# Stacking the split projections by 32 KB transfers within SBUF instead of through a DRAM scratch

## The reference, cut to what matters

```python
x = x + 0.5 * moe(layernorm(x))            # 8 experts, top 2, capacity 193
x = x + attention(layernorm(x))            # 16 heads of 8, causal, ALiBi, biases
x = x + 0.5 * moe(layernorm(x))

# attention, per sequence (S = 512, H = 16, HD = 8)
q, k, v = x @ Wq + bq, x @ Wk + bk, x @ Wv + bv
scores = einsum('bthd,bshd->bhts', q, k) / sqrt(HD) + alibi     # -inf above the diagonal
out = einsum('bhts,bshd->bthd', softmax(scores), v) @ Wo + bo
```

## Time and profile before

| | |
|---|---|
| median of 3 runs (lowest, highest) | 1023.84 us (1015.57, 1025.05) |
| the profiled execution: its time, its span | 1020.61 us, 1018.9 us |
| mean granted TensorE clock, of full speed | 0.893 |
| busy: TensorE, VectorE, ScalarE, GpSimd | 869.3, 756.3, 634.8, 537.1 us |
| all DMA | 92532 packets, 75.15 MB |
| scratch stores | x192, 128.0 KB, median 2.4 us from issue to landing |
| stack transfers | x64 each to `q_st`, `k_max`, `k_exp`, 192.0 KB, medians 3.8, 5.0 and 6.1 us |
| shift transfers | x64, 4.0 KB, median 4.0 us |

### The profile page before, as it was taken

How to read it: one execution, slowest core, us unless ns; L and a number is a source line. 1 busy time by engine, 2 the same in 40 slices (tenths; PEclk the granted TensorE clock), 3 DMA queues, 4 the chain that set the end, 5 groups by cost and what they waited for, 6 DMA issues and landing times. The chain is left out here.

```text
span 1018.9 us, 24637 instructions
## 1 busy us (share of the span) xinstructions
PE 869.3 (85%) x6498; PEld 396.8 (39%) x6498; DVE 756.3 (74%) x2534; ACT 634.8 (62%) x1538; POOL 537.1 (53%) x838
## 2 busy tenths in 40 slices
PE   4989995389798897898998988989989995998997
PEld 3444442143243343433433433433433433544443
DVE  5999984477776777778777777778777813799996
ACT  4676764007665575676676666666766783676765
POOL 3777775234453553544544544535535231677777
PEclk9999997557897898989988988988988997899999
DMA  6600000653644725535526436346247000011001
GB/s 170 95 0 0 0 0 1 155 120 77 116 98 70 147 61 96 132 66 112 121 67 122 105 68 137 89 81 140 76 80 155 2 2 22 11 31 31 27 25 42
DMA packets 92532, 75.15 MB, mean 74 GB/s; under 512 B 11540, under 2 KB 92308, under 8 KB 92308
## 3 DMA queue, kind: packets, MB, share of 16 engines
q1 hardware_dynamic: 92488, 74.63, 34.8%
HBM read 44.97 MB, written 29.36 MB: 73 GB/s over the span
## 5 line engine op out<-in xcount | busy, mean ns | idle before, releaser
L1099 DVE TENSOR_REDUCE att_neg_max<-att_max 128x1 bf16<-128x512 f32 (+3 forms) x704 | 416.3, 637 | 149.3 <-PE att_max L893 147.3
L992 ACT ACTIVATE att_probs<-att_exp 128x512 f32<-128x512 f32 x640 | 352.5, 600 | 201.2 <-PE att_exp L912 196.8
L1064 POOL TENSOR_SCALAR_AFFINE_SELECT att_probs<-att_probs 128x512 f32<-128x512 f32 x256 | 157.7, 638 | 272.1 <-ACT att_probs L992 272.1
L890 PE MATMUL att_max<-att_k_max,att_q_st 51*128 51x384 bf16 (+2 forms) x768 | 198.9, 304 | 56.4 <-DMA att_k_exp<-qk_parts 48.2
L912 PE MATMUL att_exp<-att_q_st,att_k_exp 64*128 64x512 bf16 (+3 forms) x1024 | 230.2, 326 | 4.8 <-DMA att_q_st<-att_shift 3.3
L928 PE MATMUL att_pv<-att_probs,att_v 128*32 128x512 f32 (+3 forms) x2048 | 216.2, 498 | 1.5 <-POOL att_probs L1064 1.5
L358 ACT ACTIVATE moe_scaled<-moe_hi,moe_gates 128x128 f32<-128x128 f32 x512 | 146.1, 372 | 60.6 <-PE moe_hi L304 60.3
L893 PE MATMUL att_max<-att_k_max,att_q_st 62*128 62x128 bf16 x1024 | 182.1, 233 | 0.0
L518 DVE SCALAR_TENSOR_TENSOR x<-moe_lo,moe_gates,x 128x128 f32 (+1 forms) x512 | 160.5, 338 | 19.5 <-PE moe_lo L298 18.4
L890 PEld LDWEIGHTS att_max<-att_k_max,att_q_st 51*128 51x128 bf16 x768 | 74.1, 99 | 253.8 <-DVE att_neg_max L1099 164.4
L298 PE MATMUL moe_lo<-moe_we,moe_hT 128*128 128x512 f32 x256 | 136.0, 614 | 0.0
(11 more groups left out here) (81 smaller groups left out, 892.2 us busy)
## 6 DMA issues: line engine op xcount, KB each, us to landing
qk_parts<-att_parts SPq DMA_DIRECT2D x192, 128.0 KB, 2.4
att_q_st<-qk_parts SPq DMA_DIRECT2D x64, 192.0 KB, 3.8
att_k_max<-qk_parts SPq DMA_DIRECT2D x64, 192.0 KB, 5.0
att_k_exp<-qk_parts SPq DMA_DIRECT2D x64, 192.0 KB, 6.1
x<-in_L_attn_x SPq DMA_DIRECT2D x16, 256.0 KB, 3.1
out<-x SPq DMA_DIRECT2D x16, 256.0 KB, 2.3
moe_we<-in_L_ffn_We SPq DMA_DIRECT2D x2, 512.0 KB, 4.6
att_q_st<-att_shift SPq DMA_DIRECT2D x64, 4.0 KB, 4.0
```

Of the source, the lines that this page charges most:

```text
L890: nc.tensor.matmul(max_ps[m % RING][:, at:at + width - P], q_st[par][low:low + FINE_ROW, r, i * P:(i + 1) * P], k_max[par][low:low + FINE_ ...
L992: nc.scalar.activation(probs[g % 2][:, n, :], exp_ps[m % RING][:], ACT.Exp).then_inc(exp_done, 1)
L1064: nc.gpsimd.affine_select(out=view, in_=view, compare_op=ALU.is_ge, fill=0.0, base=0, pattern=[[0, 4], [1, P]], channel_multiplier=-1).the ...
L1099: nc.vector.tensor_reduce(neg_max[par][:, g // 2, 1 - g % 2, heads[0]:heads[0] + len(heads), i], max_ps[m % RING][:, 0:len(heads) * width] ...
```

## The change

The DRAM tensor and `store_parts` go away. `stack` copies straight from `parts` to the stacks: for each half, each of the six terms, each stack and each of the two heads of a pair one transfer of 8 destination rows by 4 pairs by 512, read from 32 source rows, 36 per half and 72 per sequence. To make the 32 source rows of one half and one head of the pairs adjacent, the columns of Wq and Wk and their biases are handed over in another order. A first half waits for the split parts term by term; the first split of a sequence waits for the whole second half of the sequence before. The tables of slots are new: statistics and normalise of a sequence stand in group 3 of the step before, `turn_h`, projections and splits come earlier, `shift_hi` and `turn_o1` later. An extra step at -3 starts the first sequence.

```diff
--- before.py
+++ after.py
@@ -562,15 +562,17 @@
 
 
 SIDE_WORK = [
-    {2: "shift_hi"},
-    {1: "turn_h", 3: "turn_o1", 5: "project_q", 8: "project_k"},
-    {0: "turn_o", 3: "shift_lo", 6: "project_v"},
-    {1: "output", 3: "turn_o0"},
+    {3: "turn_h", 7: "project_q"},
+    {0: "project_k", 5: "shift_hi", 9: "turn_o1"},
+    {3: "turn_o", 7: "shift_lo"},
+    {0: "project_v", 4: "output", 9: "turn_o0"},
 ]
 
-PREPARE = {(0, 1): "statistics", (0, 2): "aggregate", (0, 3): "add_eps", (0, 4): "take_root", (0, 6): "shift_mean",
-           (0, 7): "normalise0", (0, 8): "normalise1", (0, 9): "normalise2", (0, 10): "normalise3", (1, 6): "split_q0", (1, 7): "split_q1", (1, 8): "split_q2", (1, 9): "split_q3",
-           (1, 10): "split_k0", (2, 0): "split_k1", (2, 1): "split_k2", (2, 2): "split_k3", (3, 4): "add_bias"}
+
+PREPARE = {(0, 10): "split_q0", (1, 0): "split_q1", (1, 1): "split_q2", (1, 2): "split_q3",
+           (1, 3): "split_k0", (1, 4): "split_k1", (1, 5): "split_k2", (1, 6): "split_k3", (2, 4): "add_bias",
+           (3, 0): "statistics", (3, 1): "aggregate", (3, 2): "add_eps", (3, 3): "take_root", (3, 6): "shift_mean",
+           (3, 7): "normalise0", (3, 8): "normalise1", (3, 9): "normalise2", (3, 10): "normalise3"}
 PV_AFTER = {3: 0, 5: 1, 7: 2, 9: 3}
 MAX_UNITS = 11
 EXP_UNITS = 10
@@ -657,7 +659,6 @@
 
 
 
-    scratch = nc.dram_tensor("qk_parts", [2, 2, PAIRS, 2, len(Q_PARTS), HD, S], BF16, kind="Internal").ap()
     w, q_st, k_max, k_exp, v = ops.w, ops.q_st, ops.k_max, ops.k_exp, ops.v
     bq_col, bk_col, bv_col, bo_rows = ops.bq_col, ops.bk_col, ops.bv_col, ops.bo_rows
     with ExitStack() as ctx:
@@ -707,11 +708,9 @@
         hn_done = sem("hn_done")
         bias_added = sem("bias_added")
         split_step = both(lambda s: sem(f"split_step{s}"))
-        scratch_in = both(lambda i: both(lambda s: sem(f"scratch_in{i}{s}")))
         stack_in = both(lambda i: both(lambda hf: sem(f"stack_in{i}{hf}")))
         shift_in = both(lambda i: both(lambda hf: sem(f"shift_in{i}{hf}")))
-        SCRATCH_DMAS = len(Q_PARTS)
-        STACK_DMAS = 6
+        STACK_DMAS = 2 * 3 * len(Q_PARTS)
         SHIFT_DMAS = 2
         max_out = sem("max_out")
         max_read = sem("max_read")
@@ -763,12 +762,12 @@
 
         def all_steps(eng, step):
 
-            for b in range(-2, 2):
+            for b in range(-3, 2):
                 step(b, b % 2, b // 2)
-            with eng.Fori(1, NSEQ // 2 - 1) as i:
+            with eng.Fori(1, NSEQ // 2 - 2) as i:
                 step(2 * i, 0, i)
                 step(2 * i + 1, 1, i)
-            for b in range(NSEQ - 2, NSEQ + 1):
+            for b in range(NSEQ - 4, NSEQ + 1):
                 step(b, b % 2, b // 2)
 
         def there(b):
@@ -782,8 +781,11 @@
                         on_max(b + 1, 1 - par, half + par, g, n)
                     if on_exp and n < EXP_UNITS and there(b):
                         on_exp(b, par, half, g, n)
-                    if on_prepare and (g, n) in PREPARE and there(b + 2):
-                        on_prepare(b + 2, par, half + 1, PREPARE[g, n])
+                    if on_prepare and (g, n) in PREPARE:
+                        if g < GROUPS - 1 and there(b + 2):
+                            on_prepare(b + 2, par, half + 1, PREPARE[g, n])
+                        if g == GROUPS - 1 and there(b + 3):
+                            on_prepare(b + 3, 1 - par, half + par + 1, PREPARE[g, n])
                     if on_side and n in SIDE_WORK[g] and present(b, SIDE_WORK[g][n]):
                         on_side(b, par, half, SIDE_WORK[g][n])
                     if on_pv and n in PV_AFTER:
@@ -804,7 +806,7 @@
                 eng.wait_ge(side_read, use(b - 2, "project_k" if s else "project_q"))
                 if after(b, 0):
 
-                    eng.wait_ge(scratch_in[1 - par][s], (half + par) * (SCRATCH_DMAS * DMA))
+                    eng.wait_ge(stack_in[1 - par][1], (half + par) * (STACK_DMAS * DMA))
                 eng.sem_inc(passed, 1)
                 ins = ops_of.tensor_scalar(parts[s][:, 0], qk[s][:], 1.0, 1.0, ALU.mult, ALU.mult)
             elif n == 1:
@@ -821,29 +823,21 @@
 
         @block.sync
         def _(sp):
-            def store_parts(b, par, half, side):
-
-                which = (Q_PARTS, K_PARTS)[side]
-                for term in sorted(range(len(which)), key=lambda t: which[t]):
-                    part = which[term]
-                    sp.wait_ge(split_step[side], b * 4 + (1, 3, 4)[part])
-                    sp.dma_start(scratch[par, side, :, :, term].rearrange("r u d s -> (r u) d s"),
-                                 parts[side][:, part]).then_inc(scratch_in[par][side], DMA)
-
             def stack(b, par, half, hf):
 
-                if hf == 0:
-                    for side in range(2):
-                        sp.wait_ge(scratch_in[par][side], half * (SCRATCH_DMAS * DMA) + SCRATCH_DMAS * DMA)
                 if after(b, 1):
                     sp.wait_ge(exp_out, (b - 2) * NE + (hf + 1) * NE // 2)
                 pairs = slice(hf * PAIRS // 2, (hf + 1) * PAIRS // 2)
-                for side, stacks in ((0, (q_st,)), (1, (k_max, k_exp))):
-                    for dst in stacks:
-                        for ab in range(2):
-                            sp.dma_start(dst[par][ab * SIDE:ab * SIDE + HEAD_ROWS, pairs, :],
-                                         scratch[par, side, pairs, ab].rearrange("r t d s -> (t d) r s")).then_inc(
-                                stack_in[par][hf], DMA)
+                rows = PAIRS // 2 * HD
+                for side, which, stacks in ((0, Q_PARTS, (q_st,)), (1, K_PARTS, (k_max, k_exp))):
+                    for term, part in enumerate(which):
+                        if hf == 0:
+                            sp.wait_ge(split_step[side], b * 4 + (1, 3, 4)[part])
+                        for dst in stacks:
+                            for ab in range(2):
+                                at, low = ab * SIDE + term * HD, (2 * ab + hf) * rows
+                                sp.dma_start(dst[par][at:at + HD, pairs, :],
+                                             parts[side][low:low + rows, part]).then_inc(stack_in[par][hf], DMA)
 
             def place_shift(b, par, half, hf):
 
@@ -858,8 +852,6 @@
                 if there(b):
                     place_shift(b, par, half, 1)
                 if there(b + 2):
-                    store_parts(b + 2, par, half + 1, 0)
-                    store_parts(b + 2, par, half + 1, 1)
                     stack(b + 2, par, half + 1, 0)
                 if there(b + 1):
                     place_shift(b + 1, 1 - par, half, 0)
@@ -1182,6 +1174,10 @@
     from concourse.bass_utils import run_bass_kernel_spmd
 
     arrays = {f"in_{n}": np.ascontiguousarray(inputs[n]) for n in _INS}
+    for n in ("Wq", "bq", "Wk", "bk"):
+        a = arrays[f"in_L0_attn_{n}"]
+        heads = a.reshape(-1, 2, PAIRS // 2, 2, HD).transpose(0, 3, 1, 4, 2)
+        arrays[f"in_L0_attn_{n}"] = np.ascontiguousarray(heads).reshape(a.shape)
     nc = bacc.Bacc("TRN2", target_bir_lowering=False, num_devices=1)
     args = [nc.dram_tensor(n, list(a.shape), mybir.dt.from_np(a.dtype), kind="ExternalInput").ap()
             for n, a in arrays.items()]
```

## The result

The changed kernel takes 1291.96 us (median of 4 runs, 1285.93 to 1303.38) against 1022.03 us (4 runs): ratio 1.267, interval 1.260 to 1.274. The forecast said slower and 1224 us; it is slower by a further 68 us, 2 us beyond the top of the range.

A forecast was written before the change was run, and what follows sets the result against it. The prediction took a loop of 36 SP issues (22.7), landing (2.4), POOL (10.2) and TensorE (16.5), 51.8 us a step, to bind the changed kernel; with the ends, 1020.6 + 203 = 1224 us, range 1125 to 1290.

The forecast's parts named there:

- the rival of a cheap issue: On SP, an issue under 0.19 us makes nothing late and removes 47 us of stalls: 974 us, chance 0.05.
- the price of one new issue: SP's time to issue one new transfer, 0.59 + 0.04 = 0.63 us, priced like transfers cut differently on both sides.
- my upper bound: SP's price per new issue at most 0.67 us, from the first 12 scratch stores taking 7.95 us.
- The queue: SP's own work per step, two halves of 36 issues and two shift pairs: almost full, ending at 49.7 us.
- the loop: From one second half's start to the next: 36 issues, landing, POOL, TensorE to the step's end; 51.8 us, binding.
- slower than their issue: Rival on the new DMA transfers: on 4 engines 1258 us, on 2 beyond 1600 us; chance 0.09.
- The low clock: Rival: TensorE stays at 1.2 GHz some 10 us more after each of two stalls, +70 us, 1294; chance 0.05.

The follow-up runs named there:

- the tables alone: The kernel before with only the new tables of slots and the extra step, parts still through the DRAM scratch: 951.54 us, ratio 0.932.
- The tables of forms: Three kernels adding groups of other transfer forms on SP behind the last output of the kernel before; only issue durations were read, not the time.
- the second buffer: The changed kernel with a second buffer for the split parts, so a split waits for the stack of two sequences before: 1281.58 us, ratio 1.258.
- the four more issues: The changed kernel with four more transfers of 32 rows behind each half, into a tile nobody reads: 1366.87 us, ratio 1.342.
- 24 issues: The changed kernel without the transfers into k_exp from sequence 2 on, 24 transfers per half in place of 36: 1131.66 us, ratio 1.111.
- the path alone: The changed kernel with the old tables of slots and old steps, leaving the 72 small transfers a sequence: 1294.1 us, ratio 1.270.

## Why the prediction was wrong

- **What bounds the kernel before** was read rightly in its stalls: the tables alone removed those for stacks and `hn`. What they are worth was put too low: the rival of a cheap issue took off their 47 us and stopped at 974 us, and the tables alone came out at 952, since the clock rose with them.
- **The direction** and its mechanism, 76 issues a step on SP (72 of them new) against 28, held: SP full, 36 issues on end twice a step, waits at group 2 and at the masks, POOL at the first split, all where the forecast put them.
- **The step that failed is the price of one new issue**, i = 0.63 us from the scratch store and the shift. It is 0.672 + 0.044 = 0.716, above my upper bound of 0.67 as well. I had taken "cut differently" as what makes an issue dear. The tables of forms show two conditions that each suffice, and a third property that no row of before could show, the divisor 8. Its surcharge (646 - 589 = 57 ns) and that of the cut beside it (693 - 646 = 47 ns) cover the missing 86 ns. The shift and the scratch store, at 584 and 589, both stand among the forms that pay no surcharge, so they could not show it.
- **So the other chain won.** The queue holds i 72 times and the loop 36 times. At 0.63 the loop ended 2.1 us later (51.8 against 49.7); at 0.716 the queue ends 2.4 us later (55.7 against 53.3). With the forecast's other terms the two cross where 36 issues make up 2.1 us, at 0.63 + 0.06 = 0.69 us. The working held the queue to be almost full, but used it neither for the central sum nor for the range. The loop's other terms were 1.8 us of landing (2.4 forecast), 10.2 us of POOL to the value product (10.2) and 15.5 us of TensorE (16.5). That the queue and not the loop binds is shown by the second buffer (1282 us, where the loop wanted 1150 to 1170), by the four more issues (+61 to +75 us, where the loop wanted 40 or less) and by 24 issues (44.3 us a step, the loop).
- **In sum**, against the profiled execution: step 14 starts at 1043.3 in place of 976.2 (+67: 14 steps of 4.0 us more, and step 0 at 262.7 in place of 251.0); step 14 is 2 us longer than the forecast's 43.0, and the stretch behind the start of step 15, which I had left alone, is +11: 80 us, from 1224 to 1304.
- **The range** left no room where it mattered. A price without a row was bounded by two rows that differ from it in a property I had not looked at, and 0.05 us beyond the bound is worth 72 x 0.05 = 3.6 us a step.
- **The rivals.** Cheap issue is refuted. The transfers are not slower than their issue at 32 KB (the last is seen landed 1.7 us after its issue ends, with 35 before it), but are at 64 KB with the source read twice. The low clock was there (0.76) but not on the chain within the steps; behind the start of step 15 it goes with most of the 11 us (TensorE's busy time there is 40.2 us in place of 29.8).
- **The Trainium skill's rule** (DMA: Bandwidth & Descriptors, "Issuing engines are not separate DMA queues") that initiating is usually small beside the DMA does not carry over to this case: one issue takes 672 ns, and 36 in a row take 25.8 us, against 1.7 us from the end of the last issue until its transfer is seen landed.

## What to carry to other kernels

Before a few large transfers become many small ones, multiply the count by the issue price of the queue and compare the product with the step: bytes fell by a third here and the time rose by 27%. Give a form that no row shows a range of its own, and take all its properties (both ends' places, the cut, the rows) from rows, or measure it at the end of the kernel first. And when a change bundles a new order with a new path, time each alone: the order alone gained 7% and the path alone cost 27%, and together the gain could not be seen.

## What was not expected of the hardware

The issue of a copy within SBUF takes 583 ns for 2 rows, 646 for 8, 735 for 12 or 24, and 589 to 601 for 1, 16, 32 and 128; a copy of 8 rows to or from DRAM, uncut, takes 295. Twelve copies of 64 KB with 8 destination rows and a source read twice took 1.19 us each with the landing of the last, 55 GB/s, while the kernel before, with its stacks in flight, moved 190 GB/s.
